# Running the last head group's query blocks upward instead of downward, and the steps around it in natural order

## The reference

```python
x = x + attn_a(layernorm(x))   # 16 heads of 16, causal, ALiBi bias, output projection
x = x + ffn(layernorm(x))      # 64 experts of width 64, top 8 per token, one shared expert
x = x + attn_b(layernorm(x))   # 16 heads of 16, causal, K and V through a 64-wide latent
x = x + ffn(layernorm(x))      # the same experts again
```

## Time and profile before

| what | value |
|---|---|
| runs | 2073.05, 2067.67, 2059.44 us; median 2067.67 |
| span of the profiled execution | 2063.8 us; the profile states no other time of its own |
| TensorE busy with matmuls / weight loads | 1676.5 us (81%) / 1066.9 us (52%) |
| VectorE busy | 1483.0 us (72%) |
| ScalarE busy | 1118.6 us (54%) |
| GpSimd busy | 695.4 us (34%) |

### The profile page before, as it was taken

How to read it: one execution, slowest core, us unless ns; L and a number is a source line. 1 busy time by engine, 2 the same in 40 slices (tenths; PEclk the granted TensorE clock), 3 DMA queues, 4 the chain that set the end, 5 groups by cost and what they waited for, 6 DMA issues and landing times.

```text
span 2063.8 us, 36692 instructions
## 1 busy us (share of the span) xinstructions
PE 1676.5 (81%) x12464; PEld 1066.9 (52%) x12464; DVE 1483.0 (72%) x3241; ACT 1118.6 (54%) x1975; POOL 695.4 (34%) x778
## 2 busy tenths in 40 slices
PE   4789999999778799991097999999997777889920
PEld 4544444445456577771074444444454556777710
DVE  6588888877387865884455888888773878648843
ACT  2134757567556677661042357575675567777710
POOL 6000101000157566446750001010001575564466
PEclk9777989889888999995586689798898899999965
DMA  4650040500075656664326500405000756566643
GB/s 151 154 67 1 3 64 2 64 1 2 7 271 158 187 184 192 201 201 149 92 83 143 64 2 12 52 2 63 1 2 6 268 151 187 170 186 209 204 148 115
DMA packets 123276, 217.59 MB, mean 105 GB/s; under 512 B 16380, under 2 KB 92044, under 8 KB 118812
## 3 DMA queue, kind: packets, MB, share of 16 engines
q1 hardware_dynamic: 98520, 148.10, 26.5%
q0 software_dynamic: 24576, 67.14, 11.8%
HBM read 124.20 MB, written 90.46 MB: 104 GB/s over the span
## 4 chain that ended last, share of the span: by engine, by line
PE 58%; DVE 13%; DMA 10%; POOL 7%; issue 7%; ACT 3%; SPq 1%; DVEq 0%; ACTq 0%; POOLq 0%
PE late_banks L1580 14%; PE late_banks L1538 11%; PE exp_banks L1566 8%; PE late_banks L1398 7%; PE exp_banks L1415 6%; POOL ring_t L1009 5%; DMA ring_t<-token_rows,index_t 4%; PE late_banks L1431 3%; DVE chunk_max_t L1986 3%; DMA expert_rows<-outs_t 2%; PE late_banks L1544 2%; PE late_banks L1373 2%; DVE inter_t L1870 2%; PE exp_banks L1431 2%; POOL ring_t L1004 1%
## 5 line engine op out<-in xcount | busy, mean ns | idle before, releaser
L1225 ACT ACTIVATE probs_t<-exp_banks 128x1024 f32<-128x1024 f32 (+3 forms) x640 | 538.8, 896 | 348.0 <-PE exp_banks L1566 346.7
L1986 DVE TENSOR_REDUCE chunk_max_t<-late_banks 128x1 f32<-128x512 f32 (+1 forms) x960 | 602.8, 683 | 112.2 <-PE late_banks L1538 92.0
L1084 POOL TENSOR_SCALAR_AFFINE_SELECT probs_t<-probs_t 128x512 f32<-128x512 f32 x128 | 81.2, 635 | 871.9 <-ACT probs_t L1225 871.9
L1580 PE MATMUL late_banks<-probs_t,values_t 128*32 128x512 f32 (+3 forms) x2560 | 322.8, 580 | 9.8 <-POOL probs_t L1084 9.5
L1398 PE MATMUL late_banks<-tokensT_t,fetched_t 128*128 x2048 | 302.9, 294 | 9.8 <-issue 4.4
L1009 POOL DMA_INDIRECT ring_t<-expert_rows,rows_of_t x256 | 243.6, 952 | 177.2 <-DVE x_sb_t L1884 116.8
L1004 POOL DMA_INDIRECT ring_t<-token_rows,index_t x256 | 250.7, 979 | 140.5 <-PE late_banks L1373 88.8
L1870 DVE TENSOR_TENSOR inter_t<-late_banks,silu_t 64x256 f32<-64x256 f32 x512 | 217.2, 424 | 92.7 <-ACT silu_t L1170 81.8
L1398 PEld LDWEIGHTS late_banks<-tokensT_t,fetched_t 128*128 128x128 f32 x2048 | 258.5, 198 | 40.6 <-issue 20.9
L1538 PE MATMUL late_banks<-contextT_t,Qp_t 50*128 50x512 f32 (+7 forms) x640 | 245.4, 523 | 22.4 <-DVE part_lo_t L1927 10.5
L1538 PE MATMUL late_banks<-Kp_t,Qp_t 50*128 50x512 f32 (+7 forms) x640 | 225.3, 476 | 2.0 <-DVE chunk_max_t L1986 0.9
(11 more groups left out here) (222 smaller groups left out, 1902.3 us busy)
## 6 DMA issues: line engine op xcount, KB each, us to landing
expert_rows<-outs_t SPq DMA_DIRECT2D x256, 256.0 KB
weights_t<-in_experts SPq DMA_DIRECT2D x8, 1728.0 KB, 13.0
Qp_t<-q_parts SPq DMA_DIRECT2D x36, 256.0 KB
weights_t<-in_experts SPq DMA_DIRECT2D x4, 2112.0 KB, 9.6
Kp_t<-k_parts SPq DMA_DIRECT2D x24, 256.0 KB
q_parts<-part_hi_t SPq DMA_DIRECT2D x16, 256.0 KB, 2.6
q_parts<-part_lo_t SPq DMA_DIRECT2D x16, 256.0 KB, 3.4
k_parts<-part_hi_t SPq DMA_DIRECT2D x16, 256.0 KB, 3.3
```

Source lines behind the costliest of these rows:

```text
L1225: act.activation(probs[:, e % NP, 2 * p:2 * p + 2, off:QB], exp_banks[sq % 2][:, :, off:QB], ACT.Exp, scale=D ** -0.5).then_inc(exp_done, 1)
L1580: last = pe.matmul(pv_banks[n % NPV][32 * h:32 * h + 32, off:QB], values[:, j, GH * g + h, :], probs[:, e % NP, h, off:QB], start=(j == 0) ...
L1986: op = dve.tensor_reduce(chunk_max[:, slot, p, r, c], bank[:, 0:n].rearrange("q (p k) -> q p k", p=len(parts)), AX.X, ALU.max)
```

## The change

The last group takes its blocks upward like the others. The halves of the experts, the order in which norms and transposes take their blocks, the order in which the output is stored, and an index that followed the old order are made natural: 0, 1, 2, 3. No instruction is added or taken away; the cost table of the planner stays as it was, and it writes a new order for the core of each attention.

```diff
-UP, DOWN = list(range(NB)), list(range(NB))[::-1]
-BLOCKS = [(g, b) for g in range(G) for b in (UP if g < G - 1 else DOWN)]
+UP = list(range(NB))
+BLOCKS = [(g, b) for g in range(G) for b in UP]
...
-HALVES = [range(HT, T), range(HT)]
+HALVES = [range(HT), range(HT, T)]
...
-        MIDDLE = [2, 3, 0, 1]
-        order_of = {phase: UP if not i else MIDDLE if phases[i - 1][0] == "f" else DOWN for i, phase in enumerate(phases)}
+        order_of = {phase: UP for phase in phases}
...
-                for i, b in enumerate(MIDDLE):
+                for i, b in enumerate(UP):
                     sp.wait_ge(combined, (f * T + (i + 1) * TPB) * TOPK)
                     store(b)
...
-                        for b in MIDDLE[0:2]:
+                        for b in UP[0:2]:
                             normalise(phase, b)
-            for b in MIDDLE[2:4]:
+            for b in UP[2:4]:
                 normalise(phase, b)
...
-                        dve.wait_ge(ctx_high, layer * KC * NB + DOWN.index(b) * KC + k + 1)
+                        dve.wait_ge(ctx_high, layer * KC * NB + UP.index(b) * KC + k + 1)
```

## The result

The changed kernel takes 2110.12 us (median of four runs, 2099.17 to 2133.80) against 2070.36 for the kernel before on the same chip; the ratio on record is 1.0206 [1.0156, 1.0255]. Run once more beside the first experiments it took 2107.88 us against 2065.78, 1.0182 [1.0113, 1.0251]. The change costs about 40 us, where the prediction had 25.6.

The account below looks back on a forecast made before the run. The bound was taken as VectorE's maxima up to a group's largest block, then that block's 16 units of scores. Two attentions cost 27.4 us, the joint gained 1.8; 25.6 added to 2067.67 gave 2093 us, range 2060 to 2112.

Parts of the forecast that it names:

- absorbed: Rival, chance 0.14: VectorE's 12.7 us idle takes up projections, the third follows the last maxima; 6.4 us gained, 2061.
- faster: Rival, chance 0.08: VectorE hides all projections and both of today's waits go; 31.8 us gained in all, 2036.
- clock kept: Rival, chance 0.03: TensorE, fed with maxima through the wait, keeps 2.4 GHz; 8.8 us lost, 2076.
- no change: Rival, chance 0.08: TensorE is the bound and keeps the same work; only the joint gains, 2066.
- worse: Rival, chance 0.09: no relief, all three projections at low clock, which lasts longer, no tail gain; 74.6 us lost, 2142.
- relief: VectorE's idle time in the last group's period absorbing part of the projections' delay: 6.3 us, between nothing and 12.7.
- step 3: Three projections ahead of (3,3)'s maxima on VectorE: 31.8 less 6.3 relief plus 3.2 low clock, 28.7 us later.
- step 5: Attention's tail: the wait for GpSimd goes and the last turn and projection keep full clock, 3.2 us less a layer.
- step 4: Last block (3,3), from end of its maxima to copy of its sums: 44 us, little saved by lacking company.
- Step 1: Last group's start: ScalarE's 6.31 us wait between (2,3) and its successor goes, as (3,0) with 10 maxima follows.
- Steps 2 and 3: Last group's maxima: (3,3)'s end one ordinary period, 103.8 us, after (2,3)'s, plus 28.7 for three projections ahead of them.
- Step 6: Joints between phases: nothing changes except the first projection of attention 1, whose wait goes; 1.8 us gained.

Follow-up runs that it names:

- the first experiments: First set of follow-ups, four on one chip; the changed kernel without edit, run among them, took 2107.88 us, 1.0182 of the kernel before.
- the two held kernels with the upward order: Changed kernel with the last group's projections held until the last maximum is placed, 2057.96 us; the same with them spread eight scores apart, 2057.78 us.
- the one with work in the waits: Changed kernel with projections held and spread, plus unused transposes in TensorE's tail waits: 2052.12 us, 0.9937 of the kernel before.
- the held kernel: Changed kernel with the last group's turns and projections held until the last maximum is placed: 2057.96 us, 0.9972 of the kernel before.
- the spread hold: Changed kernel with projections held until the last maximum is placed, then let in eight scores apart: 2057.78 us, 0.9984 of the kernel before.

## Why the prediction fell short

The direction and the cause were right, and the rivals "absorbed", "faster", "clock kept" and "no change" are out; "worse" had two of its parts right, no relief and no gain in the tail, and its low clock far too long. The size was too small. The steps that failed are step 3, which took off 6.3 us of relief where there was none, and step 5, which took off 3.2 us in the tail where 0.45 came. Against the 34.7 found in the changed stretches (the rest is not the change's, or not known), the forecast of 25.6 is 9.1 short: 5.4 of it in the two tails, 4.0 in the two cores, where step 4's error hides most of step 3's, less 0.4 in the joint.

- **Step 1, right.** No wait between (2,3) and (3,0).
- **Steps 2 and 3, the mechanism right, the relief wrong.** Foretold were 103.8 + 28.7 = 132.5 us; measured were 138.3 and 141.0. The price of a projection held: 3 x 10.6 = 31.8 foretold, 17.6 of work and 13.6 of waits found in the profile, 31.0 and 32.7 by taking them out, 10.5 for one alone. But the 6.3 of relief never came: what the projections cost net, 31.0, is what the profile shows of them gross, 17.6 + 13.6. Without the waits in the projections VectorE is idle 29.7 - 13.6 = 16.1 us in that period, 3.5 more than in an ordinary one, not 6.3 fewer. Part of it is not the projections': the two held kernels with the upward order and the one with work in the waits need 105.7 to 109.7 where 103.8 was taken, and once 119.2 at a clock of 0.77. So 107.3 + 31.0 stands against 103.8 + 31.8 - 6.3 + 3.2. The low clock that was priced at 3.2 for the third projection met the second instead (4.75; the clock is 0.50 from 470 to 480, just before it), and the third ran in 3.10.
- **What step 3 left out.** A projection issues an inverse root on GpSimd, and that queue also cuts the triangles of the block then in its scores. Behind the first projection two triangles stand behind the root, TensorE waits 2.00 us, the clock is 0.50 from 467 to 482, and the exponents of (3,1) take 25.1 us where the held kernel takes 17.8. The first exponent of (3,2) comes 15.6 us after its maxima instead of 5.5. The prediction saw this pile-up in the tail and let it go; it moved with the projections. How much of the maxima's delay it causes was not measured by itself.
- **Step 4, over-sized by 5.2.** From (3,3)'s maxima to its sums 38.8 and 38.6 us, not 44. Without the next group's maxima beside it the last block's exponents run in 31.8 and 32.0 us; those of (2,3), which has that company, take 36.7 and 40.7. The prediction had held that little is saved. That the company makes the difference is argued, not tested.
- **Steps 2 to 4 together** put the sums of attention 0 at 177.2 after (2,3)'s maxima, where 176.5 was foretold: two errors that cancel, by luck. Attention 1, taken as alike, had 179.6.
- **Step 5, failed.** The wait for GpSimd before the last sums went (0.47 and 0.29 us), and the last turn and projection still took 1.94 and 5.46 in both attentions. The tail gave 0.45 us a layer (5.67 against 6.13 up to the projection), not 3.2. The waits of 0.80, 0.90 and 1.46 us, which the prediction named as the reason for its low end, stayed, and the clock was 0.50 from 576.80 on; with work put in them the 3.2 came in both attentions. That such waits must lower the clock isn't shown: the last section has tails with the same waits at full clock. What decides it is open.
- **Step 6, right.** 2.2 where 1.8 was foretold: 9.82 or 9.83 us in all eleven profiles with the natural order of the halves, 12.00 in both with the old one. The experts' phases kept their length within some 3 us.

By layers: 17.0 and 19.8 measured against 13.7 in each. In attention 0 the 3.3 are 0.7 in the core and 2.7 in the tail; in attention 1 the core adds another 2.7. What remains of the 41.5, some 7 us, is the first group of attention 1 at a low clock, and the held kernel has the same stretch. Whether the changed kernel meets such stretches more often than the kernel before is open; the medians of about 40 leave room for some 5 us that no stretch here explains.

## What to carry to other kernels

Price a moved step on every in-order queue that it issues to, by who stands behind it there: here VectorE's maxima of the largest block, and GpSimd's triangles. An idle share read from an ordinary period is no store to pay a new delay from, unless the waits that make it up would go: here 12.7 us of idle time paid for none of 31. Where an order is bad because small work lands in front of the largest block, holding that work back recovered the time here without undoing the order; the same hold cost time where nobody waits for what stands behind it.

## What the hardware showed unexpectedly

The tail's clock is not set by its waits alone. With the same idle times in front of the same three steps, 0.80, 0.90 and 1.46 or 1.62 us, the changed kernel's last projection ran slow in both attentions (5.46 us, and the window from 576.80 above is at 0.50), and the spread hold's at full clock in both. TensorE's tail there:

```profile
552.88 0.63 PE L1596 MATMUL late_banks<-ident_t,sums_t 128*128 128x128 f32 x4 [0.80 <-ACT sums_t L1240]
554.40 1.06 PE L1603 MATMUL late_banks<-ident_t,context_t 128*128 128x128 f32 x8 [0.90 <-DVE context_t L2034]
557.09 3.10 PE L1437 MATMUL late_banks<-w_post_t,contextT_t 128*128 128x256 f32 x24 [1.62 <-DVE contextT_t L2042]
```

Over all profiles, four of the 22 tails without work in the waits took 3.10 or 3.11 us (the spread hold's two, and one each with the largest block third and with only the third projection held), the other 18 took 4.40 to 5.46. With transposes in the waits it was 3.13 or 3.14 in all four tails that had them. The Trainium skill, "TensorE: Matmul & The Clock Gate", section "What's actually happening", lets activity release the throttle; the four tails agree, and the window from 526.00 above, 8.96 of 10.00 us busy at 0.50 while VectorE takes maxima, shows again that the profile's busy time is not that activity. And an ordinary period that no edit touches, from the maxima of (1,3) to those of (2,3) in attention 1, took 105.2 us at a granted clock of 0.91 in the held kernel and 117.4 at 0.79 in the one with the largest block third:

```profile
1328.90:1434.10 105.20, 104.88 (x789) 50.74 (x788) 90.94 (x172) 69.00 (x84) 10.19 (x16) 0.91 0.25 32
```

```profile
1331.30:1448.70 117.40, 117.13 (x789) 55.72 (x789) 91.62 (x172) 69.29 (x84) 10.16 (x16) 0.79 0.23 28
```

A single profile's stretch can carry 12 us that no edit explains.
